# A third buffer for row tiles, stores by tile, and a new order at the head of each group in the second stage of an attention and expert kernel

## What is computed

```python
h = _layernorm(x, axis=-1) * (1 + ca) + sa
x = x + ga * _L0_attn_ref(h, L0_attn_w_qkv, L0_attn_w_proj, L0_attn_b_proj)
h = _layernorm(x, axis=-1) * (1 + cb) + sb
x = x + gb * _L0_ffn_ref(h, ...)     # router over 8 experts, the best 2 of each token
```

## Time and profile before

| what | us |
|---|---|
| median of three runs (2186.12 to 2189.9) | 2186.85 |
| the profiled execution | 2193.68 |
| its span in the profile | 2191.7 |
| PE busy over the span | 2075.7 (95%) |
| DVE busy over the span | 1328.8 (61%) |
| second stage, groups 2 to 14 (680.42 to 964.00) | 283.58 |

### The profile page before, as it was taken

How to read it: one execution, slowest core, us unless ns; L and a number is a source line. 1 busy time by engine, 2 the same in 40 slices (tenths; PEclk the granted TensorE clock), 3 DMA queues, 4 the chain that set the end, 5 groups by cost and what they waited for, 6 DMA issues and landing times.

```text
span 2191.7 us, 42601 instructions
## 1 busy us (share of the span) xinstructions
PE 2075.7 (95%) x9416; PEld 1625.1 (74%) x9417; DVE 1328.8 (61%) x3179; ACT 792.1 (36%) x1493; POOL 804.3 (37%) x622
## 2 busy tenths in 40 slices
PE   6999999999988999984999999999999999999997
PEld 4888878888745666653788888888888778888885
DVE  7655555555368888873565555656565555555654
ACT  3444434444345666651222222222222222222222
POOL 5676646676415666652111111111111111111111
PEclk9999999999989999986999999999999999999998
DMA  8766555655545676766955558558775965865554
GB/s 274 257 195 207 179 194 168 207 172 204 197 147 195 224 263 226 261 231 213 236 128 129 126 129 239 133 124 235 203 174 126 290 165 128 236 133 125 129 108 79
DMA packets 293820, 404.79 MB, mean 185 GB/s; under 512 B 50648, under 2 KB 188888, under 8 KB 285920
## 3 DMA queue, kind: packets, MB, share of 16 engines
q1 hardware_dynamic: 166016, 258.78, 37.2%
q0 software_dynamic: 30096, 72.12, 16.2%
q10 hardware_dynamic: 97488, 71.77, 10.4%
HBM read 210.57 MB, written 191.98 MB: 184 GB/s over the span
## 4 chain that ended last, share of the span: by engine, by line
PE 49%; DMA 2%; issue 1%; SPq 1%; DVE 0%; ACTq 0%; ACT 0%; POOL 0%; DVEq 0%; POOLq 0%
PE bank L1804 49%; DMA act_rows<-hact 1%; DMA arow<-act_rows 1%; DMA wbuf<-expert_split 0%; DMA out_rows<-orow,cur_tok 0%; SPq L566 0%; ACTq L1066 0%; DMA expert_rows<-rows,dest 0%; ACT x_t_hi L1048 0%; DVE x_t_lo L1650 0%; DMA meta<-expert_rows 0%; SPq L564 0%; DVE orow L1709 0%; POOL out_rows L791 0%; SPq L573 0%
## 5 line engine op out<-in xcount | busy, mean ns | idle before, releaser
L1804 PE MATMUL bank<-wbuf,x_t_hi 128*128 x2168 | 685.3, 397 | 30.0 <-DVE x_t_lo L1650 27.7
L791 POOL DMA_INDIRECT out_rows<-orow,cur_tok x135 | 209.0, 1548 | 969.5 <-DVE orow L1709 772.6
L1804 PEld LDWEIGHTS bank<-wbuf,x_t_hi 128*128 128x128 f32 x2168 | 410.2, 189 | 129.7 <-issue 31.8
L1804 PE MATMUL bank<-wbuf,x_t_lo 128*128 x1084 | 430.0, 397 | 0.0
L1804 PE MATMUL bank<-wbuf,act_t_hi 128*128 x1072 | 340.1, 398 | 10.4 <-DVE act_t_lo L1667 6.1
L1656 DVE TENSOR_TENSOR hact<-bank,gact 128x512 f32<-128x512 f32 x135 | 93.3, 691 | 382.0 <-PE bank L1804 361.9
L1804 PEld LDWEIGHTS bank<-wbuf,act_t_hi 128*128 128x128 f32 x1072 | 203.0, 190 | 61.0 <-issue 12.9
L1804 PEld LDWEIGHTS bank<-wbuf,x_t_lo 128*128 128x128 f32 x1084 | 205.2, 189 | 49.1
L1804 PE MATMUL bank<-wbuf,act_t_lo 128*128 x536 | 213.0, 397 | 0.0
L1048 ACT ACTIVATE x_t_hi<-bank 128x512 fp32r<-128x512 f32 x135 | 80.9, 599 | 295.4 <-PE bank L1804 281.0
L1072 ACT ACTIVATE act_t_hi<-bank 128x512 fp32r<-128x512 f32 x132 | 79.0, 598 | 276.0 <-DMA arow<-act_rows 206.8
(11 more groups left out here) (230 smaller groups left out, 3878.2 us busy)
## 6 DMA issues: line engine op xcount, KB each, us to landing
wbuf<-expert_split SPq DMA_DIRECT2D x24, 1536.0 KB
act_rows<-hact ACTq DMA_DIRECT2D x135, 256.0 KB
xrow<-expert_rows SPq DMA_DIRECT2D x538, 64.0 KB
arow<-act_rows ACTq DMA_DIRECT2D x536, 64.0 KB
expert_split<-split_hi SPq DMA_DIRECT2D x32, 768.0 KB, 3.4
expert_split<-split_lo SPq DMA_DIRECT2D x32, 768.0 KB, 5.9
q_rows<-qf SPq DMA_DIRECT2D x16, 1024.0 KB, 6.8
qb<-q_rows SPq DMA_DIRECT2D x16, 1024.0 KB
```

Of the source, the lines that this page charges most:

```text
L791: pool.indirect_dma_start(out=out, out_offset=bass.IndirectOffsetOnAxis(cur_tok[at][:, 0:1], 0), in_=orow[at % 2][:, :], in_offset=None, c ...
L1804: last = mm(dst, stationary(a, f), moving(b, f), start=(first and k == 0), stop=(k == parts * n - 1))
```

## The change

`wproj_f` becomes a view of the first 2048 floats of a new buffer `rows2` (2112 floats in each partition), and `rows2` is the third place in `rows`; `dest` gets a third place too. Group `g` uses place `g % 3`. `normed(g, t)` now waits for the scatter of tile `t` of group `g - 3`. In group 2, the first that writes `rows2`, DVE also waits until the products that read `wproj_f` are done, and POOL in group 1 clears the columns behind the 512 channels after the same wait.

`x1` is stored tile by tile (256 KB each), with a semaphore for each tile; `residual(g, t)` waits for the store of the same tile of group `g - 1`. In SP's list the order of a group is now: store tile 0, store tile 1, load queries of `g + 2`, store tile 2, load rows of `g + 1`, store tile 3. The rows' load was for `g + 2` and stood behind the store of the whole group.

In DVE's list the head of a group is now `residual(g, 0)`, `rms_var(g - 1)`, `recip(g + 1)`, `rms_seed_squared(g - 1)`, `rms_seed_error`, `residual(g, 1)`. In ACT's list `off_squared(g, 0)` stands ahead of `rms_seed(g - 1)`.

```diff
-    wproj_f = sb(keep, "wproj_f", [P, FC, C], F32)
+    rows2 = sb(keep, "rows2", [P, TPG, ROW], F32)
+    wproj_f = rows2[:, :, :].rearrange("p t r -> p (t r)")[:, 0:FC * C].rearrange("p (f n) -> p f n", f=FC)
...
     rows = [sb(ph2, f"rows{i}", [P, TPG, ROW], F32) for i in range(2)]
+    rows.append(rows2)
...
-            more = has(g, 2)
-            if more:
-                load_q(g + 2, par)
-            sp.wait_ge(s_x1, TPG * (g + 1))
-            sp.dma_start(group_rows(out, g), x1[:, :, :]).then_inc(s_x1st, 16)
-            if more:
-                load_x(g + 2, par)
+            for t in range(TPG):
+                if t == 2 and has(g, 2):
+                    load_q(g + 2, par)
+                if t == 3 and g and has(g, 1):
+                    load_x(g + 1, 1 - par)
+                sp.wait_ge(s_x1, TPG * g + t + 1)
+                sp.dma_start(out[g * GT + t * P:g * GT + (t + 1) * P, :], x1[:, t, :]).then_inc(s_x1st[t], 16)
...
+            if g == 1:
+                pool.wait_ge(s_mp, B * HG)
+                pool.memset(rows2[:, :, C:], 0.0).then_inc(s_free, 1)
+                pool.wait_ge(s_free, 3)
             number_rows(g, par)
...
+            off_squared(g, 0)
             if before_it:
                 rms_seed(g - 1)
-            off_squared(g, 0)
-            if before_it:
                 h2t_copy(g - 1, 0)
...
             dve.wait_ge(s_y, TPG * g + t + 1)
-            dve.wait_ge(s_x2, 16 * (g + 1))
             if t == 0:
-                at_least(dve, s_x1st, 16 * g)
+                dve.wait_ge(s_x2, 16 * (g + 1))
+            at_least(dve, s_x1st[t], 16 * g)
...
-            at_least(dve, s_scat[t], SCAT * (g - 1))
+            at_least(dve, s_scat[t], SCAT * (g - len(rows) + 1))
...
+            if g == len(rows) - 1:
+                dve.wait_ge(s_mp, B * HG)
...
+            residual(g, 0, par)
             if router:
                 rms_var(g - 1)
-            residual(g, 0, par)
-            if router:
-                rms_seed_squared(g - 1)
             if not last:
                 recip(g + 1)
             if router:
+                rms_seed_squared(g - 1)
                 rms_seed_error()
             residual(g, 1, par)
```

More of the change, by code:

```diff
@@ L230, in build @@
     rn, rrn = (sb(ph2, f"sum_{i}", [P, TPG], F32) for i in range(2))
-    dest = [sb(ph2, f"dest{i}", [P, 2, TPG], U32) for i in range(2)]
+    dest = [sb(ph2, f"dest{i}", [P, 2, TPG], U32) for i in range(len(rows))]
     cnt, ntl, cend = (sb(ph2, f"cnt_{i}", [P, E], F32) for i in range(3))
@@ L296, in build @@
         sem("kvp_ready"), sem("kvp_hi_ready"), sem("kvp_lo_ready"), sem("sel_ready"))
-    s_q2, s_x2, s_x1st = sem("q_back"), sem("x_back"), sem("x1_stored")
+    s_q2, s_x2, s_x1st = sem("q_back"), sem("x_back"), [sem(f"x1_tile{t}_stored") for t in range(TPG)]
     s_den, s_aden, s_rec0, s_dene, s_rec, s_rb, s_on = (
@@ L387, in batch_of, with rows_of @@
         return g // GPB
+    def rows_of(g):
+        return rows[g % len(rows)]
     def phase1_over(eng):
@@ L758, in number_rows @@
                 wait_apart(pool, s_rowm, 2 * g)
[L759 removed]
+            pool.tensor_copy(rows_of(g)[:, :, TOK_AT].bitcast(I32), tok_no[:, :]).then_inc(s_rowm, 1)
             wait_apart(pool, s_rowm, 2 * g + 1)
@@ L769, in scatter @@
                 for k in range(2):
-                    pool.indirect_dma_start(out=xs, out_offset=bass.IndirectOffsetOnAxis(dest[par][:, k, t:t + 1], 0),
-                                            in_=rows[par][:, t, :], in_offset=None).then_inc(s_scat[t], 16)
+                    pool.indirect_dma_start(out=xs, out_offset=bass.IndirectOffsetOnAxis(dest[g % len(rows)][:, k, t:t + 1], 0),
+                                            in_=rows_of(g)[:, t, :], in_offset=None).then_inc(s_scat[t], 16)
         def group2(g, par):
@@ L953, in square @@
                 at_least(act, s_var3, g)
-            act.activation(sq_out[:, :], rows[par][:, t, 0:C], ACT.Square, accum_out=ss[:, t:t + 1]).then_inc(s_sq, 1)
+            act.activation(sq_out[:, :], rows_of(g)[:, t, 0:C], ACT.Square, accum_out=ss[:, t:t + 1]).then_inc(s_sq, 1)
         def h2t_copy(g, t):
@@ L1466, in places_chosen, with destinations @@
             turn.did(tt(chosen[:, :, :, :], pos[:, :, :].unsqueeze(1).to_broadcast([P, 2, TPG, E]), oh[:, :, :, :], ALU.mult), "chosen")
-        def destinations(par):
+        def destinations(g):
             turn.after("chosen")
             with nc.allow_low_precision("row numbers under 2 ** 24, whole in both types"):
-                dve.tensor_reduce(dest[par][:, :, :], chosen[:, :, :, :], AX.X, ALU.add).then_inc(s_dest, 1)
+                dve.tensor_reduce(dest[g % len(rows)][:, :, :], chosen[:, :, :, :], AX.X, ALU.add).then_inc(s_dest, 1)
         def all_places(g, par):
@@ L1476, in all_places @@
             places_chosen()
-            destinations(par)
+            destinations(g)
         def choice(g):
@@ L1550, in group2 @@
                 next_places()
-                destinations(1 - par)
+                destinations(g - 1)
             rstd2_of(1)
@@ L1972, in turn_h2 @@
             for f in range(FC):
-                last = pe.transpose(H2_B[t % 2][:, f * P:(f + 1) * P], rows[par][:, t, f * P:(f + 1) * P], ident[:, :])
+                last = pe.transpose(H2_B[t % 2][:, f * P:(f + 1) * P], rows_of(g)[:, t, f * P:(f + 1) * P], ident[:, :])
             last.then_inc(s_h2t, 1)
```

14 lines of the change are left out of this document (8 added, 6 removed).

## The result

The changed kernel took 2245.62 us (median of four runs, 2232.49 to 2252.12), beside 2186.48 us of the kernel before (four runs, 2184.25 to 2189.9): ratio 1.0262, 95% interval 1.0231 to 1.0293. It is 59 us slower, where 2167 had been forecast. Every one of its four runs lies above the forecast's range.

The account below looks back on a forecast made before the run. PE was taken as the bound, held by DVE, which DMAs delay. 9.5 + 2.6 - 1.6 + 8.8 = 19.3 us, plus 0.7 for groups 1 and 15, made 20 off 2186.85: 2167 us (2160 to 2173).

Parts of the forecast that it names:

- The head of the group: Start of each group: `residual(g, 0)` waits for nothing ahead, so PE's 9.5 us of waits for `rec` go (other bound 7).
- The third place: `normed`'s 16.1 us of DVE waits for scatters go, and with them PE's 2.6 us for `mkb` (bounds 0 and 2.6).
- Stores by tile: DVE's 2.5 us wait for the store of `x1` goes, already counted in `rec`; no cost on the path.
- Rival D: Rows' load comes too late, each `residual(g, 0)` 2.2 us late, 22.5 us a group: 2197 us; chance 0.06.
- The fixed 2.0 us a DMA: Rows' load behind one small store: estimated 2 us longer, 6 of the 9.1 us available, so it still fits.
- DVE can follow: Second stage: DVE sheds 2.2 us a group and can go round in 19.6 us against PE's 20.3.
- Rival C: DVE's instructions stretch beside POOL's, and DVE sets the pace near 21.5 us a group: 2183 to 2187 us; chance 0.11.
- the copy of the logits: PE's wait for ACT's copy grows from 6.2 to 7.8 us: 1.6 us lost (bounds 1.6 lost, 6.2 gained).
- 8.8 us of clock: PE's clock falls, seen in five of thirteen groups, go as its stops shrink: 8.8 us gained (bounds 0 and 8.8).
- its last sentence: Sign of failure: the first wait moves elsewhere at the same length, above all to the first product waiting for `on_lo`.
- the floor of 19.7: PE's time in groups 2 to 14 without waits and clock loss: 256.5 us, 19.7 us a group.
- rival A: All of PE's second-stage waits close, including 6.2 us for the logits' copy: 29 us gained, 2158 us; chance 0.17.

Follow-up runs that it names:

- the hold of 3.4 us: Two extra ACT copies ahead of the fourth copy of the transposes: 2258.34 us on the changed kernel, 2248.58 us on the kernel before.
- the third profile: The changed kernel run a third time, with nothing altered: 2163.38 us, ratio 0.993 to the kernel before.

## Why the prediction was wrong

*The head of the group* came out as worked out: `rec` 9.5 to 0.2 us in the first profile of the changed kernel, 0 to 0.8 in the later ones. *The third place*: `mkb` 2.6 to 0.5 (in the later profiles 5.5 and 6.8 before, 1.8 to 1.9 changed), no wait of `normed` for scatters. That the third place is what removes them was too narrow; moving the transfers does it alone. *Stores by tile*: no wait for a store, and none for rows. Rival D did not come: no wait of DVE for `xb` in any profile, and the four stores of 256 KB, with the loads, gain 0.43% by themselves. The rule that I had weighed in favour of D, the one of the Trainium skill's page DMA: Bandwidth & Descriptors, section "Bandwidth", on 1 MiB and more, speaks of the share of peak bandwidth that a transfer reaches. No run here measured that, and it did not decide this case: no engine waits for these four small stores, and the kernel that has them is not slower. The fixed 2.0 us a DMA that I had taken from the same page is its fit for DMAs issued from GpSimd, while SP issues the rows' load. *DVE can follow*: 17.8 us busy in 19.8, and PE, at 19.66 of 19.79 us, is the bound. Rival C did not come.

*The clock and the copy of the logits* are the steps that failed. The prediction saw in the earlier trace rows that ACT, idle for 1.35 us, began its copy of the logits a microsecond after they had ended, at the moment when the spreads ended, and put this down to a fixed feature of the place: "Nothing in the change touches that". It was the visible end of the late signals: an idle engine, one producer, the producer done, and no start. A later profile of the same kernel has no such gap. As a lateness that varies, it should have been asked of each of PE's other consumers: what if the copies of the transposes get it, by 2 to 4 us, rather than the copy of the logits by 1? They stand straight ahead of PE's next need, and the answer is the hold of 3.4 us: some 26 us a group. The sum had -1.6 us for the copy of the logits, with bounds of -1.6 and 6.2, and no term at all for the copies of the transposes; measured, PE's wait for those is 26.4 us. It took 8.8 us of clock as a gain, with bounds of 0 and 8.8, and so left out that the clock could come to cost more than before; measured, it costs some 42 us where it had cost 8.8. The forecast had no rival for a first wait that moves to the logits; its last sentence had such a move, at the wrong place (`on_lo`).

Where signals are not late, the forecast holds, and on the rival's side of it: 2160.6 to 2170.3 us on four chips, within its range, 19.8 us a group, nearly the floor of 19.7 and the group time of rival A, with PE's wait for `lg_t` gone. Two errors of size lie in it and cancel. In the stage there was less to gain than 20 us, for the kernel before takes 274 to 276 us in groups 2 to 14 there, not 283.6, and the gain is 274.4 - 258.5 = 15.9 on the one chip and 276.0 - 258.8 = 17.2 on the other where both were profiled. And it was counted from 2186.85, while the kernel before takes 2176.3 to 2182.6 at these places. So that the time falls within the range is in part luck.

What is shown: the stop of PE at the logits, with the fall of the clock behind it, makes the loss in groups 2 to 14, and a hold of ACT's copies alone reproduces it. What is not: why PE's signals were late in the first runs. They appear in both kernels there and in none of the seventeen profiles taken on the five chips later, so they go with the place, the time or its condition. That the transposes' came 4 to 5 us late in the changed kernel and in time or 1 to 2 us late in the kernel before may come from the moved transfers, from where the transposes now stand beside the scatters, from the other spacing of its work, or from a difference between their moments. The experiments that would tell it, the loads at their old places, met no such place, and none moved or thinned the scatters. With one profile of each kernel in which signals are late, it is also not shown that the change as such is the worse one in such a condition; what the four timed runs of the changed kernel show is that it was 59 us slower there.

## What to carry to other kernels

An idle engine that starts a microsecond or more after its only producer ended, or a wait that the profile calls remote, is a sign worth a rival of its own: ask of every consumer on the critical engine's path what a lateness of 2 to 4 us there would cost, clock included, before taking its removal for granted. A stop that is cheap at 0.8 us can cost over ten times as much at 2.5 us, once each group's clock falls, so cover for the critical engine's inputs should be counted in microseconds of lateness that it can bear. And where a gain of 0.7% on four chips stands against a loss of 2.6% in another comparison of the same two kernels, neither comparison alone settles the matter.

## What was not expected of the hardware

- The time from the modelled end of a matmul to the start of an idle engine that waits for it is not constant: 2.2 us for the third product in group 8 of the first profile of the changed kernel, and 5.1 us for the transposes of tile 3, against none that shows in the third profile. DMA share at these moments was 0.94 and 1.01, so a high share by itself does not bring it.
- With a stop of 2.49 us in a group PE ran at 1.2 GHz for 6.8 to 10.2 us of each, though it was busy for 311.83 of the 344.03 us. With a stop of 0.76 us in every group it stayed at 2.4 GHz. In between the rows don't agree on one bound: in group 5 of the changed kernel's first profile the stop was 1.63 us and the clock 1.00, in group 5 of the kernel before it was 1.65 us and 0.92.

```profile
750.20 1.06 PE L1993 MATMUL bank<-h2t,rw 128*32 128x512 f32 x8 [1.63 <-ACT h2t L967]
```

- The kernel before is itself 0.2 to 0.5% faster at the later places (2176.3 to 2182.6 us against 2186.48), and its groups 2 to 14 take 7.6 to 9.1 us less in its two later profiles (276.0 and 274.4 against 283.58).
